# Causal attention stage of a fused kernel on one core: compact key strips, 32-row score matmuls, another order of the steps

## The reference, cut to what matters

```python
k, q, v = (einsum('bte,fe->btf', x, W).reshape(B, T, 16, 8) for W in (Wk, Wq, Wv))
k = layernorm(k, kln_g, kln_b) * 128 ** -0.25      # over the 8 features of a head
q = layernorm(q, qln_g, qln_b) * 128 ** -0.25
dot = where(causal, -inf, einsum('bihd,bjhd->bhij', q, k))
out = einsum('bhij,bjhd->bihd', softmax(dot), v).reshape(B, T, 128)
x = layernorm(x + einsum('bte,fe->btf', out, Wo) + bo)
```

## Time and profile before

| | |
|---|---|
| median of three runs | 1454.51 us |
| the profiled execution: its span, from the first to the last instruction | 1454.0 us |
| what its runs take around the span (median less span) | 0.5 us |
| TensorE / VectorE / ScalarE / GpSimd busy | 79% / 57% / 38% / 23% |
| mean granted TensorE clock over the span | 0.894 of full speed |

### The profile page before, as it was taken

The page is one execution under the profiler, slowest core; times in us unless marked ns, Lnnn a source line. Parts: engine busy times, 40 slices in busy tenths (PEclk is TensorE's granted clock), DMA queues, the critical chain, the costliest instruction groups (busy, mean ns, idle before and its releaser), DMA issues.

```text
span 1454.0 us, 18728 instructions
## 1 busy us (share of the span) xinstructions
PE 1143.2 (79%) x6656; PEld 685.5 (47%) x6656; DVE 821.8 (57%) x2090; ACT 555.6 (38%) x1126; POOL 329.0 (23%) x229
## 2 busy tenths in 40 slices
PE   1998588978835889979949967887888267999895
PEld 0466356656623344444525644564566133444443
DVE  0766588588687454521246747775786865444303
ACT  1731255355413344432127305543553134444310
POOL 1234444144230000000022445423444000000001
PEclk9886699989976899999978858999999688999998
DMA  7000000010000000000000001000000000000000
GB/s 300 1 0 1 15 20 20 3 25 23 5 0 1 0 1 1 1 0 0 6 26 1 1 0 27 16 13 15 20 20 1 0 1 0 1 1 1 0 0 15
DMA packets 9998, 21.15 MB, mean 15 GB/s; under 512 B 1328, under 2 KB 5424, under 8 KB 9264
## 3 DMA queue, kind: packets, MB, share of 16 engines
q1 hardware_dynamic: 9184, 11.54, 3.1%
q10 hardware_dynamic: 720, 8.38, 1.4%
HBM read 11.42 MB, written 1.05 MB: 9 GB/s over the span
## 4 chain that ended last, share of the span: by engine, by line
PE 64%; DVE 19%; ACT 5%; issue 5%; DMA 2%; POOL 2%; POOLq 1%; SPq 0%; DVEq 0%; ACTq 0%
PE bank L589 8%; PE bank L667 8%; PE bank L314 5%; PE bank L347 5%; PE bank L452 5%; PE bank L573 5%; PE bank L362 4%; PE bank L411 4%; PE bank L554 3%; DMA x_tokens<-x_dram 2%; PE bank L475 2%; PE bank L485 2%; DVE arena L887 2%; PE bank L659 2%; ACT arena L1143 2%
## 5 line engine op out<-in xcount | busy, mean ns | idle before, releaser
L1143 ACT ACTIVATE arena<-bank 128x512 f32<-128x512 f32 (+4 forms) x324 | 159.3, 535 | 283.6 <-PE bank L314 238.8
L314 PE MATMUL bank<-consts_sb,arena 128*128 128x128 f32 x960 | 138.0, 285 | 107.1 <-DVE arena L1022 50.0
L1378 POOL TENSOR_TENSOR rstd<-vareps,neghalf 128x1 f32<-128x1 f32 x96 | 54.4, 567 | 707.2 <-DVE vareps L725 706.8
L314 PEld LDWEIGHTS bank<-consts_sb,arena 128*128 128x128 f32 x960 | 110.5, 147 | 140.1 <-DVE arena L1022 51.2
L1039 DVE TENSOR_REDUCE arena<-bank 128x1 f32<-128x384 f32 (+3 forms) x176 | 109.5, 640 | 113.6 <-PE bank L556 112.6
L1317 ACT ACTIVATE arena<-bank 128x512 f32<-128x512 f32 (+1 forms) x176 | 97.7, 559 | 159.7 <-PE bank L576 157.1
L1413 POOL TENSOR_TENSOR arena<-arena,neghalf 128x16 f32<-128x16 f32 x32 | 93.3, 2914 | 216.6 <-DVE arena L889 216.6
L589 PE MATMUL bank<-arena 128*32 128x256 f32 (+3 forms) x512 | 135.4, 447 | 0.0
L573 PE MATMUL bank<-q_strips_shifted,k_strips 128*128 128x512 f32 (+3 forms) x256 | 91.4, 411 | 33.1 <-ACT q_strips_shifted L1143 29.5
L667 PE MATMUL bank<-arena,weights 128*128 128x512 f32 x256 | 110.2, 592 | 0.0
L573 PEld LDWEIGHTS bank<-q_strips_shifted,k_strips 128*128 128x128 f32 x256 | 45.1, 201 | 123.8 <-DVE arena L1039 52.9
(11 more groups left out here) (166 smaller groups left out, 2010.0 us busy)
## 6 DMA issues: line engine op xcount, KB each, us to landing
arena<-arena SPq DMA_DIRECT2D x56, 130.0 KB, 2.3
weights<-wts_dram ACTq DMA_DIRECT2D x1, 2824.0 KB, 27.0
weights<-wts_dram ACTq DMA_DIRECT2D x1, 1817.0 KB, 20.8
weights<-wts_dram ACTq DMA_DIRECT2D x1, 1561.0 KB, 16.7
consts_sb<-consts_dram SPq DMA_DIRECT2D x1, 1296.5 KB, 9.9
rowconsts<-rows_dram ACTq DMA_DIRECT2D x1, 1088.0 KB, 10.1
x_tokens<-x_dram SPq DMA_DIRECT2D x4, 256.0 KB, 15.9
out_dram<-x_inner SPq DMA_DIRECT2D x16, 64.0 KB, 1.5
```

Source lines behind the costliest of these rows:

```text
L314: mm = pe.transpose(bank[:, i * P:(i + 1) * P], src, ident)
L1143: return act.activation(dst, src, ACT.Copy)
```

## The change

- **Strips of keys.** kS [128 x 512] holds the four heads' strips as they come out of the transpose, in three buffers instead of two. A score matmul reads 32 partitions of qS or qS2 and of kS, those of its head, so it uses 32 rows of the array.
- **Fills.** A fill is two heads (p = 0 or 1) in a pair of banks, one head per bank, of 512 or 256 columns each. Six fills make a pass of a unit; three pairs (banks 0 to 5) go round over both passes. Bank 6 serves all transposes and projections, bank 7 the values.
- **Masks.** The identity and the masks lie as four 32-row pieces in each strip (a table of 1536 columns, loaded at the start into the arena and converted by GpSimd). A diagonal block of a head takes four matmuls of 32 rows and 128 columns.
- **Readers.** VectorE reduces and ScalarE exponentiates both banks of a pair in one instruction. `values` runs per group of tiles, all four heads of a tile one after another.
- **Preparation.** The projection weights of q and k are centred on VectorE at the start of window layer 1, so no mean is taken; ScalarE copies and squares the projections; gains and biases come scaled from a table. For the second image GpSimd applies them. Its projection, statistics and strips are spread over the steps of units 0 to 2.
- **Order.** One loop over steps f on each engine: pass A fill f, pass B fill f - 8, and the rest at steps given by tables.

```diff
+        A_GROUPS = [[(3, 0)], [(0, 0), (2, P)], [(1, 0)]]
+        B_GROUPS = [[(0, 0)], [(1, 0), (3, 3 * P)], [(2, 0)]]
+        NF = 6
+        LAST = NF * G
+        def fill_of(f):
+            return f // NF, f % NF // 2, f % 2
+        def b_fill_at(f):
+            i = f - NF - 2
+            return i if 0 <= i < LAST else None
+        Q2_AT = {NF * (u + 1) + 1: u for u in range(G)}
+        Q_AT = {NF * u + 3: u + 1 for u in range(G - 1)}
+        K_AT = {NF * u + 4: u + 1 for u in range(G - 1)}
+        V_AT = {NF * (u + 1) + 2 + 2 * i + 1 + 2: (u, i) for u in range(G) for i in range(3)}
+        OUT_AT = {NF * (u + 1) + 10: u for u in range(G)}
+        PROJECT_AT = {1: 4, 2: 5, 5: 6, 6: 7}
+        STATS_AT = {2: 4, 3: 5, 6: 6, 7: 7}
...
+                def next_pair(key, until):
+                    i = filled[0] % 3
+                    filled[0] += 1
+                    for n in range(2):
+                        take(pe, (key, n), until, bank=2 * i + n)
...
+                def masked(bank, h, col, table):
+                    rows = slice(32 * h, 32 * h + 32)
+                    for j in range(NT):
+                        mm = pe.matmul(bank[:, col:col + P], strip_masks[rows, 0, j, :], strip_masks[rows, table, j, :],
+                                       start=False, stop=(j == NT - 1), skip_group_check=True)
+                    return mm
+                def fill_a(f):
+                    u, group, p = fill_of(f)
...
+                    i = next_pair(("A", f), [(mx_ready, f + 1)])
+                    for n in range(2):
+                        h = 2 * p + n
+                        rows = slice(32 * h, 32 * h + 32)
+                        for t, at in A_GROUPS[group]:
+                            pe.matmul(psum[2 * i + n][:, at:at + (t + 1) * P], qS[rows, u % 2, t * P:(t + 1) * P],
+                                      kS[rows, u % 3, 0:(t + 1) * P], start=(at == 0), stop=False,
+                                      skip_group_check=True)
+                    for n in range(2):
+                        for t, at in A_GROUPS[group]:
+                            mm = masked(psum[2 * i + n], 2 * p + n, at + t * P, 1)
+                    mm.then_inc(pe_A, 1)
...
+                    for t, at in B_GROUPS[group]:
+                        for h in range(4):
+                            mm = pe.matmul(psum[7][32 * h:32 * h + 32, t * P:S], vp[:, 4 * b + t, 4 * quad + h, :],
+                                           PT3[group][:, h, at:at + (NT - t) * P],
+                                           start=(t == 0), stop=(t == 2), skip_group_check=True)
...
+                for f in range(END):
+                    if f < LAST:
+                        fill_a(f)
+                    if f == 0:
+                        features3(1)
+                    if f in PROJECT_AT:
+                        pe.wait_ge(xT_ready, 4)
+                        project(PROJECT_AT[f], 6)
+                    if f in Q2_AT:
+                        shifted_strips(Q2_AT[f])
+                    if b_fill_at(f) is not None:
+                        fill_b(b_fill_at(f))
+                    if f in V_AT:
+                        values(*V_AT[f])
...
                 def stats3(g):
...
+                    dve.wait_ge(sq3_ready, g + 1)
+                    dve.tensor_reduce(ss, sq3[:, g % 2], AX, ALU.add).then_inc(ss3_read, 1)
+                    dve.wait_ge(ss3_read, g + 1)
+                    link(dve.tensor_scalar(var3[:, g % NT, :], ss, 1.0 / D3, EPS, ALU.mult, ALU.add))
...
+                    for t, at in A_GROUPS[group]:
+                        ins = dve.tensor_reduce(mx3[:, u % 2, t, 2 * p:2 * p + 2], scores[:, :, at:at + (t + 1) * P],
+                                                AX, ALU.max)
...
+                def weights(f):
+                    u, group, p = fill_of(f)
+                    act.wait_ge(pe_B, f + 1)
+                    if u:
+                        act.wait_ge(pe_V, 3 * (u - 1) + group + 1)
+                    wide = 512 if group < 2 else 256
+                    act.activation(PT3[group][:, 2 * p:2 * p + 2, 0:wide], pair_view(place["B", f])[:, :, 0:wide],
+                                   ACT.Exp).then_inc(E_ready, 1)
...
+            pool.wait_ge(strips_loaded, 16)
+            pool.tensor_copy(strip_masks[:].rearrange("p k j d -> p (k j d)"),
+                             arena[:, STAGING:STAGING + STRIPS_WIDTH]).then_inc(masks_ready, 1)
```

More of the change, by code:

```diff
@@ L527, in causal @@
             def causal():
[L528 to L537, removed]
-                    b, quad = divmod(u, 4)
-                    pe.wait_ge(strips_ready, NT * (b + 1))
-                    pe.wait_ge(hi_placed, NT * (b + 1))
-                    for name, src, done, until in (
-                            ("qS", QS, pe_qS, [(qS_ready, u + 1)]),
-                            ("kS", KS, pe_kS, [(kxa_ready, u + 1), (kxd_ready, u + 1)])):
-                        bank = take(pe, (name, u), until)
-                        transposes(bank, [src[:, 4 * b + t, 4 * quad:4 * quad + 4, :].rearrange("p h r -> p (h r)")
-                                          for t in range(NT)]).then_inc(done, 1)
@@ L579, in values, with project @@
-                def values(u, j):
-                    b, quad = divmod(u, 4)
-                    t, h, n, wide = PASS_B[j]
-                    i = NB * u + j
-                    if j == 0:
+                filled = [0]
+                def project(g, bank):
+                    b, t = divmod(g, NT)
+                    bank = take(pe, ("qkv3", g), [(v3_ready, g + 1)], bank=bank)
+                    pe.matmul(bank[:, 0:384], hT[:, b, tile(t)], w_("qkv3"), start=True, stop=True)\
+                        .then_inc(pe_qkv3, 1)
@@ L863, in window_layer @@
                     dve.wait_ge(tables_ready, 1)
+                else:
+                    centre_weights()
                 first = LN2 + G * l
@@ new lines, in causal @@
+                for f in range(END):
+                    if f == 0:
+                        features(3, 1)
+                    if f in STATS_AT:
+                        projected(STATS_AT[f])
+                    if f in HIGH_AT:
+                        place_high(HIGH_AT[f])
+                    if f in Q2_AT:
+                        shifted_strips(Q2_AT[f])
+                    if b_fill_at(f) is not None:
+                        weights(b_fill_at(f))
+                    if f in OUT_AT:
+                        head_outputs(OUT_AT[f])
+                    if f in Q_AT:
+                        q_strips(Q_AT[f])
+                    if f in K_AT:
+                        k_strips(K_AT[f])
+                    if f == GATHER_AT:
```

420 lines of the change are left out of this document (203 added, 217 removed).

## The result

The changed kernel takes 1471.0 us (median of six runs, 1462.0 to 1472.9) beside 1454.35 us for the kernel before on the same chip (1450.6 to 1455.7). The ratio is 1.010, with a 95% interval of 1.0074 to 1.0126: it is slower by 1%. The forecast was 1366 us, its range ended at 1450. It was wrong in its sign.

What follows compares the result with a forecast made beforehand. TensorE was taken as the bound in units, VectorE in the preparation. Per iteration 37.7 us saved in units and 7.5 in preparation, twice 90.4, less 2 added elsewhere, took 1454.5 to 1366 us; range 1330 to 1450.

Steps and rivals of the forecast that it cites:

- 3.0 us per step: Causal stage: a unit is six steps, 18.0 us against 20.4; 40 middle steps were priced at this.
- rival 4: Causal stage: the clock falls because a quarter of the array is a light load; near 1550 us, chance 0.03.
- (a): Value matmuls: four heads in a row run side by side, 2.5 us per unit instead of 7.7, saving 5.2.
- (b): Score matmuls on 32 rows: two heads nearly side by side, 4.3 us per unit, saving 2.6.
- rival 2: Score matmuls: strips of rows do not overlap, 3.0 us more per unit, 1414 us, chance 0.13.
- (c): Mask matmuls: 128 per unit on 32 rows at 0.060 us each, 7.7 us, costing 5.8 more.
- Rivals 1 and 3: Masks: weight load partly exposed, 0.085 us each, 1417 (chance 0.15); or load plus columns, 0.13 each, 1509 (chance 0.10).
- (d): Transposes in a unit: 16 as before, 1.8 us.
- (e): TensorE changes between strips of rows, strips of columns and full array: about 12 per unit, 1.2 us.
- (f): TensorE waits for a free pair of banks: 0.5 us per unit.
- Rival 6: Causal stage: savings turn into waits for pairs of banks and nothing is left, 1450 us, chance 0.03.
- Rival 5: Causal stage: all strips overlap fully and no change costs; 14 us per unit, about 1310 us, chance 0.08.

Runs made afterwards that it cites:

- rows128: The changed kernel with every score and mask matmul on all 128 rows instead of 32 (not the reference's computation): 1375.8 us, one run.
- filler_2x512: The changed kernel plus two full-array bf16 matmuls of 512 columns ahead of each fill, 24 per unit: 1448.4 us, one run.
- old_grouped_values: The kernel before, with the value matmuls of its first two key tiles issued as four heads in a row: 1362.4 us, ratio 0.935.
- masks_rows128: The changed kernel with the mask matmuls alone on 128 rows, four per block as before, scores on 32 rows: 1386.8 us, one run.
- full_masks: The changed kernel with each diagonal block masked by one 128-row matmul, 32 per unit instead of 128: 1350.2 us, ratio 0.927 to the kernel before.
- full_masks_warm: One 128-row mask matmul per block in the changed kernel, plus 40 full-array matmuls of 512 columns ahead of the first strips: 1348.3 us, ratio 0.927.
- full_masks_warm72: One 128-row mask matmul per block in the changed kernel, plus 72 full-array matmuls of 512 columns ahead of the first score: 1404.9 us.
- after_warm72: The changed kernel plus 72 full-array matmuls of 512 columns ahead of the first score: 1468.8 us, one run.
- interleaved_masks: The changed kernel with the masks of a fill's two heads issued by turns, same instructions: 1443.1 us, ratio 0.990 to the changed kernel.

## Why the prediction was wrong

The failed step is the clock: "granted clock 1.00" in a step of the middle, and with it the 3.0 us per step. A step took 3.9 us (23.6 for six) at 0.50. The prediction priced every term of the settled unit at full clock and gave rival 4 a chance of 0.03 because in the settled unit before "value matmuls fill a quarter of the array half the time" at 1.00. Those use all 128 rows and 32 columns; rows128 differs from the changed kernel only in rows and runs at 1.00. So a quarter of the columns was no evidence for a quarter of the rows. (Nor is it half the time: 7.7 of 20.4 us by the prediction's own sum.) Rival 4's mechanism, the clock in the stage, is what happened. Its 1550 was too high twice over: the mask and score terms that it started from were, and at the low clock the masks took 1.5 times as long and the scores 1.7 times, while only the values and transposes about doubled.

Term by term, per unit, in us: the forecast; at full clock, from start to start in filler_2x512; and in the changed kernel. Each is one fill's reading times the number of such fills; neighbouring fills overlap a little, so the last column adds up to 24.3 where the unit is 23.6.

```
                forecast   at full clock                          as it ran, clock 0.50
masks, 128        7.7      4 x (0.33 + 0.78 + 0.33) = 5.8         4 x (0.41 + 1.41 + 0.41) = 8.9
scores, pass A             2 x (0.34 + 0.40 + 0.23) = 1.9         2 x (0.60 + 0.70 + 0.38) = 3.4
scores, pass B             2 x (0.34 + 0.35 + 0.23) = 1.8         2 x (0.60 + 0.58 + 0.38) = 3.1
  both            4.3      3.8                                    6.5
values            2.5      2.5 (0.99 per 512 columns)             2.5 x 1.86 = 4.7
transposes        1.8      4 x 0.50 = 2.0                         4 x 1.05 = 4.2
changes, waits    1.7      rest 1.3                               -
unit             18.0      15.4                                   23.6
```

(a) Values: right. In old_grouped_values four heads of 512 columns take 0.99 us, from 541.29 to 542.28. The settled unit falls from 20.4 to 14.4, and the program by 92.2 us, 5.8 for each of its sixteen units, where 5.2 was said:

```profile
541.29 1.06 PE L589 MATMUL bank<-arena 128*32 128x512 f32 x8
542.28 0.44 PE L573 MATMUL bank<-q_strips_shifted,k_strips 128*128 128x384 f32 x1
```

(b) Scores: right at full clock, and nearer the bound of 3.6 than the 4.3 taken. Two heads of 512 columns take 0.34 us where one took 0.32; strips of rows do overlap, so rival 2 falls.

(c) Masks, "the term that decides": 0.049 each at full clock (0.78 for 16), below the 0.060 taken and below the 0.06 called the lower bound. Within one strip they start 0.056 apart, and the second strip's begin before the first's are through. Rivals 1 and 3 fall as mechanisms. By its sign rival 1 seemed to come true, since in the changed kernel the masks stand 0.088 apart (1.41 for 16); at full clock, in filler_2x512, they stand closer than forecast. The full-row masks of masks_rows128 and rows128 follow each other at 0.06, with new weights each. The rule that the prediction set against itself, that of the Trainium skill ("TensorE: Matmul & The Clock Gate", part 3, the mechanism) by which a weight load is hidden only under a matmul of another row group, shows in neither form: the 0.056 of one strip is hardly more than the 0.053 that 128 columns take at 2.4 GHz.

(d) Transposes, 2.0 for 1.8, and (e), (f), changes and waits, 1.3 for 1.7: right within 0.4 each.

Beside the unit: the preparation gained 6.3 us, not 7.5. At the start the tiles of x landed between 1.0 us earlier and 2.2 later than in the earlier trace rows, for +1 said. Rival 6 falls: TensorE is idle for 10.3 us of 209.4 in the units. Rival 5, units of 14 us and 1310 in all, would not have come either if 15.4 is right: with it the sum would be about 1471 - 131 = 1340, worked out and not run.

So with unit terms that sum to less than forecast the program was to come out near or below 1366, and one factor that stood in none of them, the clock, turned it into 1471. The changed kernel has 1685 matmul records in a stage where the one before had 797; at full clock that is the cheaper list, at half clock it isn't.

The best version measured is full_masks, 1350.2 us (full_masks_warm, 1348.3, can't be told from it): 0.927 of the kernel before. It is partly at the low level still. Three of its four runs lie between 1346 and 1354, and one at 1362; the runs of its relatives spread by 13 to 37 us. Which level an execution takes is not settled: neither the warm start nor more full work in the last steps nor twice the masks made it steady, and full_masks_warm72 was low in its profiled execution. All its falls stand behind waits, among them one of 0.72 us per settled unit, in which TensorE waits for VectorE ahead of a transpose. A version of full_masks without that wait is the obvious next run, and wasn't made. The changed stage with full-row scores that compute the reference (they need the zero-filled strips of the kernel before) and one mask per block wasn't tried.

## What to carry to other kernels

Price a TensorE edit at both clocks, and look at the granted clock of the stage before anything else when the result is in: a busy share near 100% is no sign that it is high. Work cut to 32 rows of the array can be shorter in each term and longer in the sum; cut the number of instructions before the rows of each (one full-row mask per block, not four on 32 rows, was worth 121 us here). Look for short waits of TensorE just before the clock falls: beside 32-row work the falls seen here all had one. And when an "after" is slow, put the rows back as an experiment, since it costs one line. Evidence from a shape that is narrow in another dimension isn't evidence for yours.

## What was not expected of the hardware

- A TensorE that was 95% busy, with scores and masks on 32 rows, was granted 0.52 over 209 us; with 128-row ones in the same order it was granted 1.00 in the settled part (1375.8 us for 1471.0).
- The clock stood at 0.50 for 160 us (434.7 to 595.1) of work at 97% busy with scores and masks on 32 rows (after_warm72). With the masks on 128 rows it rose at 445 us (masks_rows128).
- Each fall from 1.00 in the units came behind a wait of TensorE, of 0.32 us (interleaved_masks), 0.72 (full_masks) or 1.15 (the changed kernel); the stage before kept 1.00 through 1.24 us in each unit.
- Adding work made the program faster: 24 full matmuls of 512 columns per unit, 1471.0 to 1448.4.
- Between the two forms a stage can run at either level: units of 13.5 and of 20.5 us from the same code in the same execution. The Trainium skill ("TensorE: Matmul & The Clock Gate", closing table) advises to keep TensorE busy without gaps to have the high clock; a stage busy for 199.0 of 209.4 us at 0.52 doesn't agree.
- In the same page of the Trainium skill, part 3, four row tiles packed together are measured at 3.07 times the speed. A gain of that kind is seen here with two: two heads of 512 columns in 0.34 us at full clock, where one took 0.32.
